# Eight buffers and four semaphores for the running sums of a graph kernel's edge phases

## What is computed

```python
# layer 0: 4 heads of 32 channels
m = x @ W_n2m.T;  q, k, v = heads(m @ Wq.T + bq), heads(m @ Wk.T + bk), heads(m @ Wv.T + bv)
e = heads(edge_attr @ W_edge.T @ We.T)
alpha = sum(q[dst] * (k[src] + e)) / sqrt(32)          # one score per edge and head
p = segment_softmax(alpha, dst)
out = segment_sum((v[src] + e) * p, dst)               # then a gate, a projection, x1 = layernorm(x + ...)
# layer 1: one head of 256 channels, on x1
scores = sum(q[dst] * k[src]) / 16 + edge_weight * we + be
out = segment_sum(v[src] * segment_softmax(scores, dst), dst)   # then layernorms and a feed-forward net
```

## Time and profile before

| | |
|---|---|
| time, median of 3 runs | 5072.7 us (5072.0 to 5076.51) |
| the profiled execution, span from first to last instruction | 6753.4 us |
| edge phase of layer 0 in it | about 3038 us (110 to 3148) |
| edge phase of layer 1 in it | about 3015 us (3385 to 6400) |
| busy share: TensorE, VectorE, ScalarE, GpSimd | 64%, 57%, 44%, 49% |
| DMA engines, mean busy | about 50 to 60% in the edge phases |

### The profile page before, as it was taken

How to read it: one execution, slowest core, us unless ns; L and a number is a source line. 1 busy time by engine, 2 the same in 40 slices (tenths; PEclk the granted TensorE clock), 3 DMA queues, 4 the chain that set the end, 5 groups by cost and what they waited for, 6 DMA issues and landing times.

```text
span 6753.4 us, 105844 instructions
## 1 busy us (share of the span) xinstructions
PE 4299.6 (64%) x23291; PEld 3492.8 (52%) x23291; DVE 3831.3 (57%) x12902; ACT 3003.4 (44%) x6997; POOL 3308.1 (49%) x3637
## 2 busy tenths in 40 slices
PE   6555555565565566566746666666666666666698
PEld 3454554555455555454534555555554555554587
DVE  4565665666566666666734444455454444444588
ACT  1444454555454454554324444444444444444432
POOL 2545555455555455452355545554555554454355
PEclk8777777777777777777978778787888787777899
DMA  6555555555555555553446556565666665555422
GB/s 201 148 145 148 146 145 146 145 153 148 149 152 145 145 152 154 148 148 99 122 141 163 161 153 162 157 162 157 164 160 158 160 160 158 157 163 158 125 73 70
DMA packets 774181, 996.11 MB, mean 147 GB/s; under 512 B 189569, under 2 KB 559489, under 8 KB 773553
## 3 DMA queue, kind: packets, MB, share of 16 engines
q10 hardware_dynamic: 394272, 443.81, 23.8%
q0 software_dynamic: 150224, 410.39, 22.7%
q1 hardware_dynamic: 229056, 135.14, 7.5%
HBM read 862.98 MB, written 125.90 MB: 146 GB/s over the span
## 4 chain that ended last, share of the span: by engine, by line
another core or an unknown queue 22%; PE 21%; DVE 17%; issue 16%; DVEq 7%; ACTq 5%; ACT 5%; DMA 2%; POOL 2%; SPq 1%; POOLq 1%
PE ps L1377 20%; DVE rows L1009 2%; DVE score L1021 2%; DVE prod L1033 2%; ACT oh L750 2%; DVE acc L1174 2%; DMA acc_d<-acc 2%; ACT place L738 1%; ACTq L827 1%; DVE prod L1016 1%; DVEq L1233 1%; ACTq L730 1%; SPq L266 1%; DVEq L1231 1%
## 5 line engine op out<-in xcount | busy, mean ns | idle before, releaser
L637 POOL DMA_INDIRECT rows<-kv_d,src_all x1564 | 1535.2, 982 | 1543.1 <-DVE score L1021 951.0
L637 POOL DMA_INDIRECT rows<-x_d,src_all x1564 | 1487.0, 951 | 1450.5 <-DVE prod L1033 962.3
L1377 PE MATMUL ps<-place 128*128 128x256 bf16 (+2 forms) x10560 | 1459.9, 288 | 296.4 <-issue 186.8
L1377 PEld LDWEIGHTS ps<-place 128*128 128x128 bf16 (+1 forms) x10560 | 1250.9, 149 | 587.4 <-issue 317.6
L1377 PE MATMUL ps<-rows,oh 128*128 x3520 | 1093.2, 470 | 457.3 <-DVE oh L1154 340.7
L1033 DVE SCALAR_TENSOR_TENSOR prod<-rows,ps 128x256 f32<-128x256 f32 x1760 | 637.3, 418 | 906.8 <-remote 549.9
L1377 PEld LDWEIGHTS ps<-rows,oh 128*128 128x128 f32 x3520 | 797.8, 236 | 617.9 <-issue 478.8
L750 ACT ACTIVATE oh<-iota_row,rel 128x128 f32<-128x128 f32 x2640 | 837.9, 388 | 552.9 <-remote 408.8
L1377 PE MATMUL ps<-msg,oh 128*128 128x132 f32 x3520 | 607.0, 330 | 595.8 <-DVE msg L1149 331.8
L1377 PEld LDWEIGHTS ps<-msg,oh 128*128 128x128 f32 x3520 | 544.1, 235 | 638.9 <-DVE msg L1149 421.0
L738 ACT ACTIVATE place<-dst_row,node_tab 128x512 f32<-128x512 int32 (+1 forms) x880 | 613.2, 708 | 385.4 <-DVE acc L1174 145.3
(11 more groups left out here) (217 smaller groups left out, 4152.9 us busy)
## 6 DMA issues: line engine op xcount, KB each, us to landing
dst_row<-in_dst_row ACTq DMA_DIRECT2D x880, 256.0 KB
place<-q_d ACTq DMA_DIRECT2D x440, 192.8 KB
acc_d<-acc ACTq DMA_DIRECT2D x440, 128.5 KB
ea<-in_ea SPq DMA_DIRECT2D x440, 128.0 KB
acc_d<-acc ACTq DMA_DIRECT2D x440, 66.0 KB
place<-q_d ACTq DMA_DIRECT2D x440, 64.0 KB
rows<-kv_d,src_all POOLq DMA_INDIRECT x1564
rows<-x_d,src_all POOLq DMA_INDIRECT x1564
```

What stands on the lines that cost most here:

```text
L637: pool.indirect_dma_start(out=L.rows[:, t % SLOTS, j, 0:D], out_offset=None, in_=L.table, in_offset=bass.IndirectOffsetOnAxis(ap=src_all[: ...
L1377: return pe.matmul(out_, lhsT=lhsT, rhs=rhs, start=first, stop=last)
```

## The change

The running sums get eight buffers, one for each pair of a chunk, and the stores four semaphores. VectorE's accumulate now waits for the store of eight pairs ago, ScalarE's store for the one of four pairs ago. In layer 0 the buffers are slices of one new tile `acc` (8 x 132 values a partition, where there were 4 x 257); in layer 1 they lie alternately in that tile and in `msg`, which only layer 0 uses. The same four semaphores serve both layers, so the counts of layer 1 start at those of layer 0. GpSimd clears 1056 columns at the start where it cleared 257.

```diff
@@ -39,7 +39,8 @@
-ACCS = 4
+ACCS = CH
+STORES = 4
@@ -198,7 +199,8 @@
-        acc = [sb(f"acc{b}", [P, D + 1]) for b in range(ACCS)]
+        acc_space = sb("acc", [P, ACCS * (DM + HEADS)])
+        wide_space = msg_space[:, 0:ACCS // 2 * (D + 1)]
@@ -310,11 +312,11 @@
-            for x in ("gathered", "stored"):
-                s[x] = [sem(f"l{n}_{x}{b}") for b in range(2)]
+            s["gathered"] = [sem(f"l{n}_gathered{b}") for b in range(2)]
             return s
 
         s_l = [edge_sems(0), edge_sems(1)]
+        s_l[0]["stored"] = s_l[1]["stored"] = [sem(f"sums_stored{b}") for b in range(STORES)]
@@ -334,8 +336,12 @@
+        L0.stores_before, L1.stores_before = 0, 16 * NPAIR // STORES
+        L0.acc = [acc_space[:, b * L0.AW:(b + 1) * L0.AW] for b in range(ACCS)]
+        L1.acc = [space[:, b // 2 * L1.AW:(b // 2 + 1) * L1.AW] for b in range(ACCS)
+                  for space in ((acc_space, wide_space)[b % 2],)]
@@ -521,8 +527,8 @@
-                for b in range(2):
-                    sp.wait_ge(s["stored"][b], 16 * NPAIR // 2)
+                for b in range(STORES):
+                    sp.wait_ge(s["stored"][b], L.stores_before + 16 * NPAIR // STORES)
@@ -589,7 +595,7 @@
-            pool.memset(acc[(CH - 1) % ACCS][:, :], 0.0)
+            pool.memset(acc_space[:, :], 0.0)
@@ -767,10 +773,10 @@
                 def store(c, st):
-                    g, b = CH * c + st, st % 2
+                    g, b = CH * c + st, st % STORES
                     after(act, s["acc"], g + 1)
-                    after(act, s["stored"][b], 16 * (CH // 2 * c + st // 2))
-                    act.dma_start(window(L.acc_d, g), acc[st % ACCS][:, 0:L.AW]).then_inc(s["stored"][b], 16)
+                    after(act, s["stored"][b], L.stores_before + 16 * (g // STORES))
+                    act.dma_start(window(L.acc_d, g), L.acc[g % ACCS]).then_inc(s["stored"][b], 16)
@@ -1161,17 +1167,17 @@
-                    old = acc_scaled if st == 0 else acc[(st - 1) % ACCS]
+                    old = acc_scaled[:, 0:L.AW] if st == 0 else L.acc[st - 1]
                     v.wait_ge(s["agg"], g + 1)
 
-                    after(v, s["stored"][b], 16 * (CH // 2 * c + st // 2 - ACCS // 2 + 1))
-                    v.scalar_tensor_tensor(acc[st % ACCS][:, 0:L.AW], old[:, 0:L.AW], keep_tab[:, bass.ds(g, 1)], agg_ps(L, b),
+                    after(v, s["stored"][st % STORES], L.stores_before + 16 * ((g - ACCS) // STORES + 1))
+                    v.scalar_tensor_tensor(L.acc[st], old, keep_tab[:, bass.ds(g, 1)], agg_ps(L, b),
                                            ALU.mult, ALU.add).then_inc(s["acc"], 1)
```

More of the change, by code:

```diff
@@ L1163, in shrink_sums @@
                     v.tensor_tensor(acc_scaled[:, 0:L.AW].rearrange("p (h c) -> p h c", h=H),
-                                    acc[(CH - 1) % ACCS][:, 0:L.AW].rearrange("p (h c) -> p h c", h=H),
+                                    L.acc[CH - 1].rearrange("p (h c) -> p h c", h=H),
                                     rescale[:, 0:H].unsqueeze(2).to_broadcast([P, H, L.AW // H]), ALU.mult)
```

## The result

| | median us | runs |
|---|---|---|
| before | 5074.6 | 4 (5072.0 to 5088.12) |
| changed | 4890.42 | 4 (4883.95 to 4897.72) |

The ratio is 0.9629, its 95% interval 0.9615 to 0.9643: 184 us less. The forecast was 5065 and its range 5028 to 5090; the time lies 138 us under the range.

A forecast was written before the change was run, and what follows sets the result against it. No engine was taken to bound the kernel, only latency in a chunk's order. Terms of 2 + 0 + 2 + 5 + 0.6, about 10 us profiled, were carried over as 7.7 us: 5072.7 to 5065 us, range 5028 to 5090.

The forecast's parts named there:

- The step that failed: Whole kernel: the profiled execution is a slowed one, and its stretches without pauses are what the timed run consists of.
- the account of 165.3 us: Both edge phases: waits put down to landed stores, 127.5 us in layer 1 and 37.8 us in layer 0.
- The upper bound of 45 us: Whole kernel: a third of the 135 us (2%) that the chain gives to landed stores, so 5028 us at best.
- Accumulate 5 of layer 0: VectorE in layer 0: waits for store 1's landing, real and on the path, 9.5 us, half of it gained: 5 us.
- VectorE's accumulate in layer 1: Layer 1: 33.5 us of waits in 45 cases, taken to be for TensorE's matmul; value 0 to 3 us.
- ScalarE in layer 0: Layer 0: 28.3 us of ScalarE waits in 12 cases, partly TensorE's, the rest covered by slack; value 2 us.
- The sum of parts: Whole kernel: gains of the separate waits added, 2 + 0 + 2 + 5 + 0.6, about 10 us profiled.
- The boundary of layer 1: Between layer 1's chunks: ScalarE's 94.0 us of waits are really for accumulate 7, so about 2 us gained.
- Rival 1: Both layers: stores land later in the timed run, so the change pays 10 to 50 us; chance 0.31.
- The last sentence of the forecast: Whole kernel: prediction is wrong if landings in an unslowed run are over 1 us longer than in the profiled execution.
- Rival 2: Shared DMA queue: more stores on their way crowd the loads behind them, costing 23 us (5096); chance 0.13.
- The memset and the slices' starts: Kernel start: clearing 1056 columns costs 1 us more, hidden; unaligned slices need up to 24 beats for 17.

The follow-up runs named there:

- the first trace: Profiled execution of the unchanged kernel from which the forecast was made: span 6753.4 us, where the median without a profile was 5072.7 us.
- the second trace: The unchanged kernel before, profiled once more: ran in 5031.33 us, with a span of 5029.6 us.
- The buffers alone: Changed kernel's tile and slices with eight buffers but only two store semaphores in both layers, against the kernel before: ratio 0.9964.
- the place alone: Changed kernel's new tile and slices, but four buffers and two semaphores as before, against the kernel before: ratio 1.0009.

## Why the prediction was wrong, point by point

**The step that failed** is the first: that the stretches without pauses of the slowed execution "are what the timed one is made of". From it came the account of 165.3 us (241.2 by the view that gives 650.8 in an execution of the timed length) and the chain's 2% (18%). Landings in the first trace were shorter (medians 2.2 and 2.8 us against 3.2 and 4.7), at 146 to 157 GB/s instead of 202 to 223, and over half of the stores' counts had no record in it. That the pauses and the lower traffic made the landings short is argued, not shown. The upper bound of 45 us was built on the 2%, so the range could not hold the result.

**Accumulate 5 of layer 0** was the right wait, called real and on the path. Its term, 5 us from 9.5 in 21 chunks, was mis-sized: it waits 109.7 us, once in each of the 55 chunks. The landing that it was worked out with, 1.59 us, was that of the phase's last chunk, where stores are as quick in the second trace (1.59 to 1.76 us). A chunk in the middle would have been the one to read, in either trace. With ScalarE's waits these are worth 2.1% in layer 0.

**VectorE's accumulate in layer 1** was put at 0, from one wait of 1.26 us that ended with the matmul. In the second trace accumulate 6 waits 100 us for landed stores, and about half of that, 51 us, lies behind the end of TensorE's sum (from the semaphores' records). This term was not a tie to be set to nothing.

**ScalarE in layer 0** was taken to have slack (2 us from 28.3). In the second trace it waits 203.7 us there for stores (103.6 + 96.8 + 3.3), and the row at 1092.00 shows that the slack does not cover it: TensorE waits for `msg` behind a held store. The buffers alone, which take VectorE's wait away and leave this one, gain nothing in layer 0 (2205.1 us); their 0.4% comes from layer 1, as far as single executions tell.

**The sum of parts** was the wrong form. I added terms for two waits; they end at one landing, so each alone is worth 0 to 0.4% and both 3.5%.

**The boundary of layer 1** was read rightly, and the wait stays, 4.4 us at a time. But it is not put down to VectorE's accumulate after the change, as the forecast had it as a sign, and mostly still to a store (50 of 53). In the second trace of before store 7 left within 0.1 us of accumulate 7's end at 37 of 55 boundaries and within 0.12 us of store 5's landing at 21.

**Rival 1** was right in sign and mechanism: landings are longer in an unslowed run, by medians 0.9 us in layer 0 and 1.9 us in layer 1. The last sentence of the forecast named over 1 us as what would make it wrong. Its price, 10 to 50 us, came from two places of a chunk. In layer 0 alone there are five: accumulate 5 and stores 3, 5, 6 and 7, each of which left as a landing came in 46 to 52 of 55 chunks. **Rival 2** shows, but small beside the gain: ScalarE's waits for `dst_row` went from 48.2 to 61.4 us in the two phases, GpSimd's for its own gathers as above, and the stores themselves land later with four on their way (medians 4.0 and 5.5 us against 3.2 and 4.7). **The memset and the slices' starts** cost nothing that the run with the place alone can tell (1.0009).

## What to carry to other kernels

Compare the span of a profiled execution with the time of unprofiled ones before reading a wait from it. Here they differed by a third, and the landings and the chain's shares were not those of the timed runs; to profile the same kernel again was the cheapest experiment. Read a landing in the middle of a phase and not at its quiet end. Where two engines wait for the same landing through different semaphores, deepen both: each alone reads as "no effect". And a long wait named after a DMA may be that of a sum computed at that moment; compare the end of the computing instruction with the start of the waiting one, as in the earlier trace rows. When a wait is taken away without any time, look whether it stands at the next instruction of the same engine.

## What the runs showed of the hardware that I had not expected

From issue to release a store of 66 KB took 1.59 us at the quiet end of a phase and 4.5 us in one stretch in the middle, at about 202 GB/s; the median in that phase was 3.2 us. A quarter of the bytes left it at 3.1. The Trainium skill (DMA: Bandwidth & Descriptors, Anatomy of one DMA, for the GpSimd path) gives 2.0 us plus the bytes at 436 GB/s, an estimate of about 2.2 us for this store; the quiet one, issued by ScalarE, is 0.6 us under it and the one of 4.5 us twice it. Why the first profiled execution was 1680.7 us longer than its kernel's other runs stays open: no later one was (spans of 4856 to 5041 us), and nothing in its trace names the cause. What the trace does show is where it stood: of the 2853 us of waits without a releaser all but 25 ended at a semaphore of TensorE that counted over 1.5 us behind the modelled end of the matmul, and the second trace has no such wait.
